# Expert slots with three buffers: x turned three slots ahead, the result product two slots behind

## The reference, cut to what matters

```python
logits = xf @ router_w.T
topk_scores, topk_ids = jax.lax.top_k(jax.nn.softmax(logits, axis=-1), 2)
cw = (one_hot(topk_ids, 8) * (topk_scores / topk_scores.sum(-1, keepdims=True))[..., None]).sum(1)
for wg, wu, wd, w in experts:          # 8 experts, 128 -> 512 -> 128
    out += w[:, None] * ((silu(xf @ wg) * (xf @ wu)) @ wd)
```

## Time and profile before

| | us |
|---|---|
| median of three runs | 1091.06 |
| lowest and highest | 1089.53, 1092.12 |
| span of the profiled execution | 1143.6 |
| slots of stage m1, first to last `gate` | 517.55 to 651.27 |
| slots of stage m2, first to last `gate` | 990.92 to 1123.46 |

### The profile page before, as it was taken

How to read it: one execution, slowest core, us unless ns; L and a number is a source line. 1 busy time by engine, 2 the same in 40 slices (tenths; PEclk the granted TensorE clock), 3 DMA queues, 4 the chain that set the end, 5 groups by cost and what they waited for, 6 DMA issues and landing times. The chain is left out here.

```text
span 1143.6 us, 27230 instructions
## 1 busy us (share of the span) xinstructions
PE 992.5 (87%) x10390; PEld 675.0 (59%) x10390; DVE 751.2 (66%) x1507; ACT 744.4 (65%) x1507; POOL 438.1 (38%) x580
## 2 busy tenths in 40 slices
PE   5889999999999989747888978999999997688883
PEld 3333333333333335637888866878878876587883
DVE  6789999999999988872222265676666666422223
ACT  4658888888888877344444457767777765544443
POOL 3742112211222111325555334555555542455541
PEclk9879999999999999869999989999999999699997
DMA  2333111111111100611113122202114310211113
GB/s 70 96 114 98 30 32 52 34 30 30 36 52 30 30 2 2 221 44 38 38 37 110 30 75 98 75 38 75 76 75 149 111 39 2 63 38 36 38 34 124
DMA packets 42150, 68.67 MB, mean 60 GB/s; under 512 B 10088, under 2 KB 21096, under 8 KB 40104
## 3 DMA queue, kind: packets, MB, share of 16 engines
q1 hardware_dynamic: 33848, 54.07, 14.4%
q0 software_dynamic: 4992, 10.23, 3.2%
q10 hardware_dynamic: 3184, 2.63, 0.7%
HBM read 51.79 MB, written 14.68 MB: 58 GB/s over the span
## 5 line engine op out<-in xcount | busy, mean ns | idle before, releaser
L803 ACT ACTIVATE PB<-S 128x512 f32<-128x512 f32 x576 | 307.9, 597 | 71.6 <-PE S L609 66.8
L915 DVE TENSOR_REDUCE mx<-S 128x2 f32<-128x1024 f32 (+1 forms) x192 | 207.6, 1128 | 8.6 <-PE S L595 8.6
L871 POOL TENSOR_SCALAR_AFFINE_SELECT PB<-PB 128x512 f32<-128x512 f32 x128 | 79.0, 635 | 307.2 <-ACT PB L803 307.1
L1452 DVE TENSOR_TENSOR m_hs<-m_gs,m_UP 128x512 f32<-128x512 f32 x78 | 53.7, 688 | 213.2 <-ACT m_gs L1322 171.7
L644 PE MATMUL PV<-PB,VP 128*32 128x256 f32 (+2 forms) x2432 | 177.7, 379 | 0.0
L609 PE MATMUL S<-W 50*128 50x512 bf16 (+3 forms) x768 | 123.9, 328 | 4.9 <-ACT PB L803 4.2
L1250 PE MATMUL m_GP<-m_xt,m_wgu 128*128 128x128 f32 x624 | 89.3, 288 | 42.0 <-ACT m_xt L1318 38.7
L1197 POOL DMA_INDIRECT yd_rows<-m_ys,m_target x78 | 76.7, 983 | 115.5 <-DVE m_ys L1459 106.5
L1318 ACT ACTIVATE m_xt<-m_XT 128x128 f32<-128x128 f32 x78 | 21.6, 277 | 147.0 <-PE m_XT L1241 74.3
L1250 PEld LDWEIGHTS m_GP<-m_xt,m_wgu 128*128 128x128 f32 x624 | 79.7, 200 | 47.4 <-issue 47.4
L595 PE MATMUL S<-W 48*128 48x512 bf16 (+3 forms) x640 | 94.5, 326 | 13.6 <-DVE mx L911 4.9
(11 more groups left out here) (344 smaller groups left out, 1879.2 us busy)
## 6 DMA issues: line engine op xcount, KB each, us to landing
d_LQ<-l_rows SPq DMA_DIRECT2D x15, 1024.0 KB, 4.9
W<-qk_parts SPq DMA_DIRECT2D x210, 32.0 KB
qk_parts<-OT SPq DMA_DIRECT2D x24, 256.0 KB, 3.0
W<-qk_parts SPq DMA_DIRECT2D x30, 96.0 KB
W<-in_L_ffn_w_gate SPq DMA_DIRECT2D x1, 2048.0 KB, 9.4
W<-in_L_ffn_w_up SPq DMA_DIRECT2D x1, 2048.0 KB, 14.4
xn_rows<-m_XN SPq DMA_DIRECT2D x8, 256.0 KB, 2.3
W<-in_L_ffn_w_gate SPq DMA_DIRECT2D x2, 1024.0 KB, 5.4
```

The lines of the kernel that those rows point to most:

```text
L803: nc.scalar.activation(PB[:, j % NPB, :], S2[:, j % 3, :], ACT.Exp, scale=SC).then_inc(exp_done, 1)
L871: nc.gpsimd.affine_select(out=tri, in_=tri, compare_op=ALU.is_ge, fill=0.0, base=0, pattern=[[0, U], [1, P]], channel_multiplier=-1).then_ ...
L915: nc.vector.reduce_max(mx[:, g % 2, c, :, heads[0], qb], S1[:, b, :, 0:w], AX.X)\
```

## The change

Three buffers take the place of two for `xt`, `gs`, `hs`, `wgu` and `UP`; `YP` gets two banks; `GP` keeps two. PE now works through up(s), x_turn(s+3), down(s-2). Since the look-ahead grows from one slot to three, the first steps turn two slots each (`turns_in`). On ACT `silu(s)` stands ahead of `x_copy(s+3)` and `w_copy(s+3)`, and a new wait keeps `up(s)` behind `silu(s-2)`.

```diff
-        xs, xt = sb("xs", [P, XB, P]), sb("xt", [P, 2, P])
-        gs, hs = sb("gs", [P, 2, FF]), sb("hs", [P, 2, FF])
-        ys, wgu = sb("ys", [P, YB, P]), sb("wgu", [P, 2, 2, FF])
+        xs, xt = sb("xs", [P, XB, P]), sb("xt", [P, 3, P])
+        gs, hs = sb("gs", [P, 3, FF]), sb("hs", [P, 3, FF])
+        ys, wgu = sb("ys", [P, YB, P]), sb("wgu", [P, 3, 2, FF])
...
-        GP, UP = ps("GP", [P, 2, FF]), ps("UP", [P, 2, FF])
-        XT, YP = (ps(k, [P, 512]) for k in ("XT", "YP"))
+        GP, UP = ps("GP", [P, 2, FF]), ps("UP", [P, 3, FF])
+        XT, YP = ps("XT", [P, 512]), ps("YP", [P, 2, 512])
...
+        DOWN_LAG = 2
+
+        def turns_in(s):
+            turned = (s + 1,) if s < 2 else (2 * s - 1, 2 * s) if s < 4 else (s + 3,)
+            return [t for t in turned if t < SLOTS]
...
                 def up(s):
                     pe.wait_ge(w_copied, s + 1)
                     pe.wait_ge(xt_copied, s + 1)
-                    for k, H, done in ((0, GP, g_done), (1, UP, u_done)):
+                    if s >= 2:
+                        pe.wait_ge(silu_done, s - 1)
+                    for k, H, done in ((0, GP[:, s % 2], g_done), (1, UP[:, s % 3], u_done)):
...
                 def down(s, e):
                     pe.wait_ge(h_ready, s + 1)
-                    if s:
-                        pe.wait_ge(y_copied, s)
+                    if s >= 2:
+                        pe.wait_ge(y_copied, s - 1)
...
                 x_turn(0)
                 pe.wait_ge(etab_ready, 1)
-                up(0)
-                x_turn(1)
-                for s in range(SLOTS):
-                    e = pe.value_load(etab[0:1, s:s + 1], min_val=0, max_val=E - 1)
-                    if s + 1 < SLOTS:
-                        up(s + 1)
-                    if s + 2 < SLOTS:
-                        x_turn(s + 2)
-                    down(s, e)
+                for s in range(SLOTS + DOWN_LAG):
+                    if s >= DOWN_LAG:
+                        e = pe.value_load(etab[0:1, s - DOWN_LAG:s - DOWN_LAG + 1], min_val=0, max_val=E - 1)
+                    if s < SLOTS:
+                        up(s)
+                    turned = turns_in(s)
+                    if turned:
+                        x_turn(turned[0])
+                    if s >= DOWN_LAG:
+                        down(s - DOWN_LAG, e)
+                    if len(turned) == 2:
+                        x_turn(turned[1])
...
+                copied = 2
                 for s in range(SLOTS):
-                    if s + 1 < SLOTS:
-                        x_copy(s + 1)
                     silu(s)
-                    if s + 2 < SLOTS:
-                        w_copy(s + 2)
+                    for t in turns_in(s):
+                        x_copy(t)
+                        if copied < min(SLOTS, s + 4):
+                            w_copy(copied)
+                            copied += 1
...
                 for s in range(SLOTS):
                     gate(s)
-                    if s:
-                        y_copy(s - 1)
-                y_copy(SLOTS - 1)
+                    if s >= DOWN_LAG:
+                        y_copy(s - DOWN_LAG)
+                for s in range(SLOTS - DOWN_LAG, SLOTS):
+                    y_copy(s)
```

More of the change, by code:

```diff
@@ L1247, in up @@
                     pe.wait_ge(xt_copied, s + 1)
-                    for k, H, done in ((0, GP, g_done), (1, UP, u_done)):
+                    if s >= 2:
+                        pe.wait_ge(silu_done, s - 1)
+                    for k, H, done in ((0, GP[:, s % 2], g_done), (1, UP[:, s % 3], u_done)):
                         for j in range(FK):
-                            last = nc.tensor.matmul(H[:, s % 2, j * P:(j + 1) * P], wgu[:, s % 2, k, j * P:(j + 1) * P],
-                                                    xt[:, s % 2], start=True, stop=True)
+                            last = nc.tensor.matmul(H[:, j * P:(j + 1) * P], wgu[:, s % 3, k, j * P:(j + 1) * P],
+                                                    xt[:, s % 3], start=True, stop=True)
                         last.then_inc(done, 1)
@@ L1255, in down @@
                     pe.wait_ge(h_ready, s + 1)
-                    if s:
-                        pe.wait_ge(y_copied, s)
+                    if s >= 2:
+                        pe.wait_ge(y_copied, s - 1)
                     for j in range(FK):
-                        last = nc.tensor.matmul(YP[:, 0:P], hs[:, s % 2, j * P:(j + 1) * P],
+                        last = nc.tensor.matmul(YP[:, s % 2, 0:P], hs[:, s % 3, j * P:(j + 1) * P],
                                                 WD[:, bass.ds(e, 1), j, :].rearrange("p o d -> p (o d)"),
@@ L1317, in x_copy @@
                     act.wait_ge(xt_done, s + 1)
-                    nc.scalar.activation(xt[:, s % 2], XT[:, 0:P], ACT.Copy).then_inc(xt_copied, 1)
+                    nc.scalar.activation(xt[:, s % 3], XT[:, 0:P], ACT.Copy).then_inc(xt_copied, 1)
                 def silu(s):
                     act.wait_ge(g_done, s + 1)
-                    nc.scalar.activation(gs[:, s % 2], GP[:, s % 2], ACT.Silu).then_inc(silu_done, 1)
+                    nc.scalar.activation(gs[:, s % 3], GP[:, s % 2], ACT.Silu).then_inc(silu_done, 1)
                 def w_copy(s):
                     e = act.value_load(etab[0:1, s:s + 1], min_val=0, max_val=E - 1)
-                    if s >= 2:
-                        act.wait_ge(u_done, s - 1)
-                    nc.scalar.activation(wgu[:, s % 2], W3[:, 0:2 * n].rearrange("p (k e f) -> p k e f", k=2, e=E)
+                    if s >= 3:
+                        act.wait_ge(u_done, s - 2)
+                    nc.scalar.activation(wgu[:, s % 3], W3[:, 0:2 * n].rearrange("p (k e f) -> p k e f", k=2, e=E)
                                          [:, :, bass.ds(e, 1), :].rearrange("p k o f -> p k (o f)"), ACT.Copy)\
@@ L1451, in gate @@
                     dve.wait_ge(u_done, s + 1)
-                    nc.vector.tensor_tensor(hs[:, s % 2], gs[:, s % 2], UP[:, s % 2], ALU.mult).then_inc(h_ready, 1)
+                    nc.vector.tensor_tensor(hs[:, s % 3], gs[:, s % 3], UP[:, s % 3], ALU.mult).then_inc(h_ready, 1)
                 def y_copy(s):
@@ L1458, in y_copy @@
                         dve.wait_ge(ys_stored[s % YB], s // YB * 16)
-                    nc.vector.tensor_copy(ys[:, s % YB], YP[:, 0:P]).then_inc(y_copied, 1)
+                    nc.vector.tensor_copy(ys[:, s % YB], YP[:, s % 2, 0:P]).then_inc(y_copied, 1)
                 for s in range(SLOTS):
                     gate(s)
-                    if s:
-                        y_copy(s - 1)
-                y_copy(SLOTS - 1)
+                    if s >= DOWN_LAG:
+                        y_copy(s - DOWN_LAG)
+                for s in range(SLOTS - DOWN_LAG, SLOTS):
+                    y_copy(s)
                 for q in range(NQ if follow is None else 0):
```

## The result

The changed kernel takes 1092.53 us (median of 12 runs, 1091.32 to 1093.78). The kernel before, run beside it, takes 1089.66 us (12 runs, 1087.35 to 1092.12). The ratio is 1.0028, with a 95% interval of 1.0017 to 1.0039: 2.87 us slower, which is just over the 0.2% that can be told from no change. The forecast said 1092.2 us, a loss of 1.1 us and so no change that shows: the direction was right, and the loss is 2.6 times as large. That 1092.2 lies within 0.4 us of the measured 1092.53 is luck, since the forecast started from a median of three runs, 1091.06, which is 1.40 us above the median of twelve.

A forecast was written before the change was run, and what follows sets the result against it. The prediction took PE to bound the expert slots at 2.79 us each, with the pauses only in the recording. Adding 0.55 us in each of two stages, +1.1 us, to the median 1091.06 gave 1092.2 us, range 1065 to 1097.

The forecast's parts named there:

- The pauses are not in the timed runs: Expert slots: PE's pauses, 54.2 us, belong to the recorded execution, so removing them was taken to gain 0.
- The rule from the Trainium skill's "Perfetto Trace Analysis": Rival in the expert slots: pauses are real and added buffers remove them, 1038 us if all go; chance 0.23.
- remote: ACT's copy of the turned x: waits 63.9 us, 19 times, called the one line without a known releaser.
- the excess: First to last gate of m1 and m2: 27.7 + 26.5 = 54.2 us beyond thirty-eight periods of 2.79 us.
- the sharpest test: Changed kernel's profile: recorded span may shrink by tens of us as PE rides over late results, while times stay.
- Steady slots at no cost: Slots between a stage's edges: PE still has 2.79 us of work in each, so the change costs nothing.
- Gather behind scatter: POOL's queue: gather(s+9) stands behind the later scatter(s), needing 5.4 us of 8.4 us, so hidden.
- the new wait on silu: PE's up(s) waits for silu(s-2), two slots old with over 2.79 us to spare: no cost.
- The start of a stage, +0.6 us: Slot 2's gate product waits behind its turning as slot 1's does: 0.6 us, bounds 0.46 to 0.7.
- The end of a stage, -0.05 us: Three scatters follow one another at a stage's end; the last comes 0.55 us later, the start's 0.6 included.
- The clock rival: Stage starts: a second PE pause lowers the granted clock, 1095.5 us; chance 0.17 with other edge losses.

The follow-up runs named there:

- the one with fewer products: Kernel before with 16 in place of 26 of the products PE makes behind stage m1 that nobody reads: ratio 0.9996.
- the lag alone: Changed kernel's buffers and result product two slots behind, but x turned one slot ahead as in the kernel before: ratio 1.0029.
- the fetch alone: Changed kernel with the next result's expert number fetched ahead of the second turning in steps that turn two slots: ratio 1.0023.
- the lag's end alone: Result product two slots behind, x turned one ahead, result product 36 and its copy put ahead of slot 38's products: ratio 1.0015 to the kernel before.
- both together: Changed kernel with expert number fetched ahead of a second turning and result product 36 ahead of slot 38's products: 1089.43 us, ratio 1.0007.

## Why the prediction was right about the gain and short on the loss

**The pauses are not in the timed runs: right.** The forecast took nothing for them, and the buffers alone gained nothing (0.9997). The rule from the Trainium skill's "Perfetto Trace Analysis", section "Optimization Strategy", that a repeated gap can mean too few buffers, would have given 1038 us; the trace of the kernel before recorded again does not show the gaps, and no kernel with more buffers has a median below 1086 us. One reading was too narrow: "remote" is not the only wait of that view without a known releaser, since its lines marked "issue" have none either. The sum does not rest on it, because the excess was taken from the first and the last `gate`. The reason behind the number holds less far. I counted the fall of the recorded span as the sharpest test and as PE riding over late results, but the kernel before fell to 1088.4 us without any edit, so that fall tests nothing about the change.

**Steady slots at no cost: right.** They are 2.79 us apart in every recording but the first. Gather behind scatter and the new wait on silu cost nothing that shows.

**The start of a stage, +0.6 us: the mis-sized step.** Slot 2's gap came as priced (0.64 us). But I costed the look-ahead by its first two turnings alone, and passed over the two steps that turn two slots. With one bank `XT`, the second turning waits for the first one's copy, and the expert's number is fetched behind that wait: 0.47 us more, twice. The start costs 1.58 us.

**The end of a stage, -0.05 us: right.** From the last gate product to the last scatter it is 6.00 us against 5.19, and a result product of 0.89 us has moved behind that gate product: -0.08 us. The parts hold too: 1.66 us from the first result product to its scatter (1.67 forecast), 1.28 between scatters (1.29).

**A term that was missing: the stretch between the stages.** The forecast has nothing for the work behind m1. In the recordings of the changed kernel it takes 332.87 and 333.05 us, against 332.04 in the kernel before recorded again and 330.64 in the one with fewer products, with more of it at the lower clock.

So 0.55 us a stage became 1.50: 1.58 at the start and -0.08 at the end. With a first slot 0.09 us longer (5.08 us against 4.99 to slot 1's gate product) this makes the 1.58 us seen in m2. Two stages are some 3 us, which would do for the measured 2.87 (1.9 to 4.3 us by the ratio's interval). But the stretch between the stages adds 0.8 to 2.4 us in the recordings, and the lag alone lost as much time with 0.57 us at the edges of a stage. The parts of single recordings do not add up to the loss within 1 us, and even ahead of m1, where no edit reaches, they differ by more: m1's first turning comes 508.01 to 512.36 us after the start. Leaving out the first slot, the fetch alone took 0.80 us off m2 and the lag's end alone 0.39, and only both together showed clearly in the time. How the loss divides between the edges and the clock behind them stays open.

**The clock rival: fell where it was looked for.** Behind slot 2's turning the gate product takes 1.13 us, the full-clock duration, in both stages, so the second pause costs no clock there. Behind m1 the recordings do show a lower clock, by another way than this rival's. The measured 1092.53 lies well under the rival's 1095.5.

## What to carry to other kernels

Before believing a repeated pause in one recording, hold its span against the timed runs, and record the kernel once more: here 54 of 1143.6 us were of one execution. One recording is also too little to share out a loss of 3 us among parts below 1 us. A look-ahead has a price at the fill and the drain of a pipeline: walk through the first and the last steps one instruction at a time, and ask of each step that does two things what stands behind its second wait. Where PE has no idle time within a slot, a deeper pipeline has nothing to gain in the steady slots and can lose at its edges; an order that covers the first wait (here a turning between two products) can gain there. And look at the stretch that follows the changed stage as well: here it differed by 2 us, with the granted clock, although no edit of the order touched it.

## What the runs showed of the hardware

- One execution of the kernel before had PE's results reach ACT some 2.3 us late 19 times, and none of the other 13 recordings, of this kernel and its variants (spans 1083.3 to 1092.6 us), has it. What made them late stays open.
- Two scatters 1.27 us apart let the load of m1's results follow after 2.38 us, three after 3.3 to 3.8 us; behind m2 it is 2.37 us after three as well. Why three land later only behind m1 was not found. The work behind m1 begins 8.35 us after the last scatter in either case.
- A fetch of the expert's number on PE costs nothing that shows behind a product, but 0.47 us behind a turning that has to wait for a copy, and 0.84 us (0.96 against 0.12) where no product stands between the two turnings.
- The granted clock of one and the same stretch, outside the expert stages, differs between orders (0.57 to 0.79 from 16 to 24 us behind m1's last scatter) and between executions of the same kernel (1.00 and 0.79 from 304 to 312 us behind it, in the two recordings of the kernel before).
